# Third stage of a deformable convolution: every tile's corner sum kept in one tensor and transposed once

## The chip, the cores and the metric

The kernel runs on one core of one Trainium2 chip. The metric is the device time of one execution in microseconds (us); lower is better. Three executions without the profiler took 3535.86, 3537.91 and 3540.14 us, a median of 3537.91 us.

## The reference, cut to what matters

Two deformable convolutions follow each other, each with batch norm and leaky ReLU, and the input is added at the end. The first has one tap (a 1x1 kernel), the second nine (3x3). x is (8, 512, 52, 52) in float32, the middle tensor has 256 channels.

```
def _dcnv2(x, w_off, b_off, w, b, k, pad):
    om = conv(x, w_off, pad) + b_off
    oy, ox, mask = om[:, :P], om[:, P:2 * P], sigmoid(om[:, 2 * P:])
    val = bilinear(x, oy + base_y, ox + base_x) * mask      # 4 corners, weighted
    return einsum('ncphw,ocp->nohw', val, w) + b
h = bn_lrelu(_dcnv2(x, w_off1, b_off1, w1, b1, 1, 0), g1, bb1, m1, v1)
h = bn_lrelu(_dcnv2(h, w_off2, b_off2, w2, b2, 3, 1), g2, bb2, m2, v2)
return x + h
```

The bilinear value of a pixel at one tap is the sum of four corners, each corner's 256 channels times one weight.

## The kernel before, in words

The 21632 pixels are 169 tiles of 128. A first stage multiplies x with w1 (each factor split in a high and a low part) and writes table 1; a second samples table 1, makes h, writes it as table 2 and works out the offsets, corner weights and row numbers of all nine taps (plan2). Both end near 892 us of the profiled span, and the change doesn't touch them.

The third stage takes the tiles in groups of four (a super, 512 pixels) and each super in nine taps. There are 42 full supers, so 378 full taps, and then nine taps of a single tile. `r` numbers the taps. The five queues run the same list of taps (`position`, line 859): the first 18 taps (two supers) are written out, then a loop makes 20 passes of 18 taps, then the rest is written out. For one tap `r`:

- POOL gathers, for each of the four tiles, 128 rows of 4 x 256 numbers (the four corners) into one of 18 slots of `gather2` (L944). A slot comes free when DVE has made the tile's last corner step.
- ACT multiplies corner 0 by its weight into `val` (L959, four times), and for tile 2 alone corner 1 by its weight into `val_too` (L962). Between tile 1 and tile 2 it copies the transposed sums of tap r-2 out of PSUM in reduced precision: `val_hi` (L971, `upper`), once PE has transposed tap r-2 and finished the products of tap r-4.
- DVE adds the other corners with one SCALAR_TENSOR_TENSOR each (L1010, a "corner step"): first FIRST_PAIR (tiles 0 and 1, six steps), then `lower` of tap r-2 (L1017, `val_lo` = psum minus `val_hi`), then SECOND_PAIR (tiles 2 and 3, five steps). Tile 2 is summed in two parts: `val` gets corners 0 and 2, `val_too` corners 1 and 3. At taps 3 and 4 of a super two relus (L1024) and two residual adds (L1033) follow, for the super before.
- PE transposes the four tiles into `psum_val` (L1062, two halves of 128 channels each), when DVE's last step of the tap is done (`sampled`). For tile 2 each half takes two matmuls, one for `val` and one for `val_too`, and PSUM adds them up: ten instructions. Then come the 24 products of tap r-2 (L1076, `multiply`: 4 output blocks, 2 halves, 3 pairs of high and low parts) into `psum_acc`.
- When a super's nine taps are in, ACT takes the four blocks of `psum_acc` out to `z_sb` (L980, at its taps 3 and 4 of the next super, named EVACUATE), and PE's first product of the next super, in its step of tap 2, waits for that.
- SP loads plans and residual rows and stores the results.

The lines that set the order on DVE and the parts of tile 2:

```
def in_parts(r, i):
    return i == 2
FIRST_PAIR = ((0, 1), (1, 1), (0, 2), (1, 2), (0, 3), (1, 3))
SECOND_PAIR = ((3, 1), (2, 2), (3, 2), (2, 3), (3, 3))
EVACUATE = {3: {2: 0, 3: 1}, 4: {0: 2, 1: 3}}
RESIDUAL = {3: (0, 1), 4: (2, 3)}
```

A pair (i, q) is tile i, corner q.

## Time and profile before

| | before |
|---|---|
| median of 3 runs, us | 3537.91 |
| the profiled execution's own time, us | 3560.49 |
| its span, first to last instruction, us | 3558.7 |
| PE busy | 3205.6 us, 90% |
| DVE busy | 3041.0 us, 85% |
| ACT busy | 1743.8 us, 49% |
| POOL busy | 2299.7 us, 65% |
| mean granted TensorE clock | 0.964 of full speed |
| DMA | 1125.77 MB, mean 316 GB/s |

Busy is the time in which at least one instruction of the engine is under way, so it hides how close two instructions follow. The profiled execution took 22.6 us more than the median of the runs without the profiler; differences are worked out within it and then set against the median. In a timeline row "x5" are five instructions that follow without a gap; consecutive ones overlap a little, so the pace of a row "2.85 us x7" whose single instruction takes 0.48 is (2.85 - 0.48) / 6.

### The profile page before, as it was taken

Reading aid. Unit: us, or ns where it says so; the run is one execution under the profiler, and the core shown is the slowest. Engines: PE = TensorE matmul, PEld = TensorE weight load, DVE = VectorE, ACT = ScalarE, POOL = GpSimd, SP = SyncE. Lnnn points to the kernel's source line nnn. Section 1 sums busy time; section 2 is a strip of 40 time slices with the busy share of each in tenths; the row PEclk is TensorE's granted clock in tenths of the full one; section 3 lists DMA queues with packets and bytes.
Section 4 is the critical chain, followed back from the end, with each engine's and each line's share of the span. In section 5 each row is a group of like instructions: output and inputs, shape, how many; then the busy total and the mean of one; then the engine's idle time right before and its main releaser. Section 6 shows DMA issues by size and latency. Waiting matters only on the chain.

```text
span 3558.7 us, 60220 instructions
## 1 busy us (share of the span) xinstructions
PE 3205.6 (90%) x16754; PEld 2630.8 (74%) x16754; DVE 3041.0 (85%) x6454; ACT 1743.8 (49%) x3762; POOL 2299.7 (65%) x1727
## 2 busy tenths in 40 slices
PE   6996676776699999999999999999999999999999
PEld 6995443433588888888888788888878888887888
DVE  5546999998798898989898889889888988989894
ACT  3664656565344444444444444444444444444442
POOL 0002333331788788888888888878787887888781
PEclk8998988888799999999999999999999999999997
DMA  8997777775999989999999999899999989999991
GB/s 292 319 338 249 254 246 248 251 251 188 356 363 343 339 314 356 350 336 329 362 349 324 350 356 341 318 357 354 328 336 365 339 318 354 351 339 328 360 341 65
DMA packets 454538, 1125.77 MB, mean 316 GB/s; under 512 B 42812, under 2 KB 198972, under 8 KB 454256
## 3 DMA queue, kind: packets, MB, share of 16 engines
q0 software_dynamic: 244672, 891.09, 68.1%
q1 hardware_dynamic: 121520, 144.69, 12.0%
q10 hardware_dynamic: 88192, 88.61, 7.7%
q14 instruction: 139, 1.14, 0.1%
q8 instruction: 15, 0.25, 0.0%
HBM read 987.20 MB, written 137.04 MB: 316 GB/s over the span
## 4 chain that ended last, share of the span: by engine, by line
PE 64%; issue 4%; DVE 3%; ACT 2%; ACTq 0%; DMA 0%; DVEq 0%; POOL 0%; POOLq 0%
PE psum_acc L1076 55%; PE psum_val L1062 10%; DVE val L1010 2%; ACT val_too L962 1%; ACT val L959 1%; ACT z_sb L980 1%; DVE val_lo L1017 1%; DMA gather<-table,plan_in 0%; ACTq L979 0%; DMA plan_in<-plan 0%; POOL gather L944 0%; DVE val_too L1010 0%; ACTq L977 0%; ACT val_hi L971 0%; DVEq L1006 0%
## 5 line engine op out<-in xcount | busy, mean ns | idle before, releaser
L944 POOL DMA_INDIRECT gather<-table,plan_in x1521 | 2092.2, 1376 | 545.1 <-issue 347.4
L1010 DVE SCALAR_TENSOR_TENSOR val<-gather,plan_in,val 128x256 f32<-128x256 f32 x3807 | 1580.2, 476 | 122.7 <-ACT val L959 90.2
L1076 PE MATMUL psum_acc<-val_hi,w_hi 128*128 128x512 f32 (+1 forms) x3096 | 1241.5, 401 | 58.2 <-ACT z_sb L980 58.2
L1076 PE MATMUL psum_acc<-val_hi,w_lo 128*128 128x512 f32 (+1 forms) x3096 | 1214.3, 392 | 0.0
L1076 PE MATMUL psum_acc<-val_lo,w_hi 128*128 128x512 f32 (+1 forms) x3096 | 1209.7, 391 | 0.0
L971 ACT ACTIVATE val_hi<-psum_val 128x1024 fp32r<-128x1024 f32 (+1 forms) x387 | 391.7, 1012 | 1382.7 <-PE psum_acc L1076 1382.7
L1076 PEld LDWEIGHTS psum_acc<-val_hi,w_hi 128*128 128x128 f32 x3096 | 592.3, 191 | 174.8 <-ACT z_sb L980 65.2
L959 ACT ACTIVATE val<-gather,plan_in 128x256 f32<-128x256 f32 x1521 | 694.5, 499 | 27.1 <-DMA gather<-table,plan_in 27.0
L1076 PEld LDWEIGHTS psum_acc<-val_hi,w_lo 128*128 128x128 f32 x3096 | 591.3, 191 | 120.6
L1076 PEld LDWEIGHTS psum_acc<-val_lo,w_hi 128*128 128x128 f32 x3096 | 592.8, 191 | 108.2
L1017 DVE TENSOR_TENSOR val_lo<-psum_val,val_hi 128x1024 fp32r<-128x1024 f32 (+1 forms) x387 | 464.8, 1201 | 202.8 <-ACT val_hi L971 201.7
L1062 PE MATMUL psum_val<-ident,val 128*128 128x128 f32 x3042 | 484.7, 275 | 59.2 <-DVE val L1010 59.2
L1062 PEld LDWEIGHTS psum_val<-ident,val 128*128 128x128 f32 x3042 | 381.3, 142 | 116.2 <-DVE val L1010 34.2
L576 POOL DMA_INDIRECT area_b<-table,row_cur x169 | 197.2, 1167 | 324.5 <-DVE area_a L726 282.8
L665 ACT ACTIVATE area_b<-psum_t 32x384 f32<-32x384 f32 (+2 forms) x594 | 259.5, 437 | 135.9 <-PE psum_t L602 123.8
L602 PE MATMUL psum_t<-area_a,area_c 128*96 128x386 f32 (+2 forms) x792 | 270.4, 479 | 22.8 <-ACT area_b L665 20.8
L339 PE MATMUL psum_t<-w_hi,val_hi 128*128 128x260 f32 x676 | 201.3, 298 | 43.6 <-DVE val_lo L463 43.1
L602 PEld LDWEIGHTS psum_t<-area_a,area_c 128*96 128x96 f32 x792 | 126.8, 174 | 137.8 <-issue 67.4
L463 DVE TENSOR_TENSOR val_lo<-area_a,val_hi 128x512 fp32r<-128x512 f32 x169 | 115.5, 691 | 128.7 <-ACT val_hi L357 128.7
L726 DVE SCALAR_TENSOR_TENSOR area_a<-area_b,area_c,area_a 128x256 f32<-128x256 f32 x507 | 206.0, 478 | 0.0
L339 PE MATMUL psum_t<-w_lo,val_hi 128*128 128x260 f32 x676 | 195.7, 290 | 0.0
L339 PE MATMUL psum_t<-w_hi,val_lo 128*128 128x260 f32 x676 | 195.5, 289 | 0.0
(74 smaller groups left out, 2327.0 us busy)
## 6 DMA issues: line engine op xcount, KB each, us to landing
stage<-x SPq DMA_DIRECT2D x70, 512.0 KB, 6.6
out<-stage SPq DMA_DIRECT2D x140, 256.0 KB, 4.0
area_a<-x SPq DMA_DIRECT2D x68, 384.0 KB, 6.4
gather<-table,plan_in POOLq DMA_INDIRECT x1521, 6.4
table<-y_stage ACTq DMA_DIRECT2D x26, 896.0 KB, 6.7
table<-area_a ACTq DMA_DIRECT2D x26, 896.0 KB, 5.6
table<-y_stage ACTq DMA_DIRECT2D x26, 768.0 KB, 6.2
table<-area_a ACTq DMA_DIRECT2D x26, 768.0 KB, 5.8
```

What stands on the lines that cost most here:

```text
L339: last = nc.tensor.matmul(y_bank(j), a[:, X_SLOT[j], k, :], b[:, k, :], start=(k == 0 and a is x_hi and b is w1_hi), stop=(k == KT1 - 1 an ...
L576: nc.gpsimd.indirect_dma_start(gather1[:, j % SLOTS, :, :].rearrange("p q c -> p (q c)"), None, table1, bass.IndirectOffsetOnAxis(ap=row_c ...
L602: last = nc.tensor.matmul(conv_bank(u, n), woff_sb[:, kt, y, :], h_t[:, kt, at:at + n * P + 2], start=(kt == 0), stop=(kt == KT2 - 1))
L665: last = nc.scalar.activation(q_sb[rows, y, 0:n * P], conv_bank(3 * b + y, n)[rows, dx:dx + n * P], ACT.Copy)
L726: ins = nc.vector.scalar_tensor_tensor(out=v, in0=gather1[:, j % SLOTS, q, :], scalar=weights1[:, q, ds(nth, 1)], in1=bias1 if q == 0 else ...
L944: nc.gpsimd.indirect_dma_start(gather2[:, slot(r, i), :, :].rearrange("p q c -> p (q c)"), None, table2, bass.IndirectOffsetOnAxis(ap=row. ...
L959: last = nc.scalar.activation(val[:, r % VALS, i, :], gather2[:, slot(r, i), 0, :], ACT.Identity, scale=weight(r, i, 0))
L971: nc.scalar.activation(val_hi[:, r % 2, :, 0:n], psum_val[:, r % 2, :, 0:n], ACT.Identity).then_inc(hi_ready, 1)
L1010: nc.vector.scalar_tensor_tensor(out=v, in0=gather2[:, slot(r, i), q, :], scalar=weight(r, i, q), in1=v, op0=ALU.mult, op1=ALU.add).then_i ...
L1017: nc.vector.tensor_tensor(val_lo[:, r % 2, :, 0:n], psum_val[:, r % 2, :, 0:n], val_hi[:, r % 2, :, 0:n].bitcast(f32), ALU.subtract)\
L1062: last = nc.tensor.matmul(psum_val[:, r % 2, kt, i * P:(i + 1) * P], v, ident[:, :], start=(n == 0), stop=(n == len(parts) - 1), is_transp ...
L1076: last = nc.tensor.matmul(psum_acc[:, oc, 0:n], a[:, w, oc * P:(oc + 1) * P], b[:, r % 2, kt, 0:n], start=(w == 0 and a is w2_hi and b is ...
```

## The change

Tile 2 is treated as the other three. ACT no longer makes `val_too`; DVE makes three corner steps for tile 2, all into `val`, so SECOND_PAIR has six steps and each waits for the one before it on the same tile; PE transposes tile 2 with two instructions in place of four. The tensor `val_too` goes. Over the 378 full taps this is one corner step more on DVE, one scaling less on ACT and two transposing matmuls (with their weight loads) less on PE, each per tap. The nine taps of the last single tile are as before.

```
-        val_too = sb("val_too", [P, VALS, C_MID])
...
-            def in_parts(r, i):
-                return i == 2
...
-            SECOND_PAIR = ((3, 1), (2, 2), (3, 2), (2, 3), (3, 3))
+            SECOND_PAIR = ((2, 1), (3, 1), (2, 2), (3, 2), (2, 3), (3, 3))
...
-                    last = nc.scalar.activation(val[:, r % VALS, i, :], gather2[:, slot(r, i), 0, :],
-                                                ACT.Identity, scale=weight(r, i, 0))
-                    if in_parts(r, i):
-                        last = nc.scalar.activation(val_too[:, r % VALS, :], gather2[:, slot(r, i), 1, :],
-                                                    ACT.Identity, scale=weight(r, i, 1))
-                    last.then_inc(scaled, 1)
+                    nc.scalar.activation(val[:, r % VALS, i, :], gather2[:, slot(r, i), 0, :],
+                                         ACT.Identity, scale=weight(r, i, 0)).then_inc(scaled, 1)
...
-                        part = in_parts(r, i)
-                        if q == 1 or part and q == 2:
+                        if q == 1:
                             dve.wait_ge(scaled, units_to(it, r, i))
-                        elif not part:
+                        else:
                             dve.wait_ge(summed, count + sums.index((i, q - 1)) + 1)
-                        v = val_too[:, r % VALS, :] if part and q == 3 else val[:, r % VALS, i, :]
+                        v = val[:, r % VALS, i, :]
...
-                            parts = [val[:, r % VALS, i, ch]] + [val_too[:, r % VALS, ch]] * in_parts(r, i)
-                            for n, v in enumerate(parts):
-                                last = nc.tensor.matmul(psum_val[:, r % 2, kt, i * P:(i + 1) * P], v, ident[:, :],
-                                                        start=(n == 0), stop=(n == len(parts) - 1),
-                                                        is_transpose=True)
+                            last = nc.tensor.transpose(psum_val[:, r % 2, kt, i * P:(i + 1) * P],
+                                                       val[:, r % VALS, i, ch], ident[:, :])
```

PE's order at the place where the products of one tap end (L1076) and the transposes of the next follow (L1062), before:

```order
L1076 MATMUL psum_acc<-val_hi,w_lo 128x512
L1062 MATMUL psum_val<-ident,val 128x128 x5
L1062 MATMUL psum_val<-ident,val_too 128x128
L1062 MATMUL psum_val<-ident,val 128x128
L1062 MATMUL psum_val<-ident,val_too 128x128
L1062 MATMUL psum_val<-ident,val 128x128 x2
L1076 MATMUL psum_acc<-val_hi,w_hi 128x512
```

and with the change, in the loop (line numbers are those of the changed file; the ISA and REGISTER rows compute what a wait compares with):

```order
L1064 MATMUL psum_acc<-val_hi,w_lo 128x512
L1045 REGISTER_ALU
L1047 REGISTER_ALU
L1051 MATMUL psum_val<-ident,val 128x128 x8
L1060 ISA
L1064 MATMUL psum_acc<-val_hi,w_hi 128x512
```

Ten transposing instructions have become eight; nothing else on PE moved.

DVE's order around the second tap with relu and residual (L1024, L1033), before:

```order
L1010 SCALAR_TENSOR_TENSOR val<-gather,plan_in,val 128x256
L1024 SCALAR_TENSOR_TENSOR z_sb<-z_sb 128x512 x2
L1033 TENSOR_TENSOR stage<-z_sb,stage 128x512 x2
L1010 SCALAR_TENSOR_TENSOR val<-gather,plan_in,val 128x256 x6
L1017 TENSOR_TENSOR val_lo<-psum_val,val_hi 128x1024
L1010 SCALAR_TENSOR_TENSOR val<-gather,plan_in,val 128x256 x3
L1010 SCALAR_TENSOR_TENSOR val_too<-gather,plan_in,val_too 128x256
L1010 SCALAR_TENSOR_TENSOR val<-gather,plan_in,val 128x256 x7
L1017 TENSOR_TENSOR val_lo<-psum_val,val_hi 128x1024
```

and with the change:

```order
L1001 SCALAR_TENSOR_TENSOR val<-gather,plan_in,val 128x256 x6
L1015 SCALAR_TENSOR_TENSOR z_sb<-z_sb 128x512 x2
L1024 TENSOR_TENSOR stage<-z_sb,stage 128x512 x2
L1001 SCALAR_TENSOR_TENSOR val<-gather,plan_in,val 128x256 x6
L1008 TENSOR_TENSOR val_lo<-psum_val,val_hi 128x1024
L1001 SCALAR_TENSOR_TENSOR val<-gather,plan_in,val 128x256 x12
L1008 TENSOR_TENSOR val_lo<-psum_val,val_hi 128x1024
```

Between two `lower` instructions twelve corner steps stand where eleven stood; the relus and residual adds keep their place.

## Rows read from the trace of the kernel before

**Rows 1.** Windows, all engines: us, busy (count), PEclk, DMA share, GB/s.

```profile
1500.00:1800.00 300.00, 289.49 (x1490) 242.89 (x1489) 266.74 (x564) 142.62 (x281) 247.23 (x174) 1.00 0.93 338
```

**Rows 2.** The page's chain that ended last, shares by engine.

```profile
PE 64%; issue 4%; DVE 3%; ACT 2%; ACTq 0%; DMA 0%; DVEq 0%; POOL 0%; POOLq 0%
```

**Rows 3.** PE in order of time, two ordinary taps: start us, us.

```profile
2201.23 0.71 PE L1062 MATMUL psum_val<-ident,val 128*128 128x128 f32 x5
...
2207.81 0.71 PE L1062 MATMUL psum_val<-ident,val 128*128 128x128 f32 x5
```

**Rows 4.** The chain in order of time, the same tap: start us, us.

```profile
2202.49 5.48 PE psum_acc L1076 x24
2207.97 1.09 PE psum_val L1062 x10
```

**Rows 5.** DVE in order of time, the same tap: [idle before, releaser].

```profile
2202.49 1.23 DVE L1017 TENSOR_TENSOR val_lo<-psum_val,val_hi 128x1024 fp32r<-128x1024 f32 x1 [0.94 <-ACT val_hi L971]
...
2205.28 2.85 DVE L1010 SCALAR_TENSOR_TENSOR val<-gather,plan_in,val 128x256 f32<-128x256 f32 x7
```

**Rows 6.** DVE in order of time, from one pass of the loop to the next.

```profile
2258.34 2.46 DVE L1010 SCALAR_TENSOR_TENSOR val<-gather,plan_in,val 128x256 f32<-128x256 f32 x6 [4.92 <-ACT val L959]
2260.73 1.21 DVE L1017 TENSOR_TENSOR val_lo<-psum_val,val_hi 128x1024 fp32r<-128x1024 f32 x1
...
2266.22 1.21 DVE L1017 TENSOR_TENSOR val_lo<-psum_val,val_hi 128x1024 fp32r<-128x1024 f32 x1
```

**Rows 7.** Who waited for whom, 1500 to 3000 us: us, times, longest.

```profile
DVE val L1010 <- ACT val L959: 55.7, 33, 4.9
DVE val L1010 <- issue: 11.6, 3, 4.0
```

**Rows 8.** PE in order of time, the same passage.

```profile
2255.48 0.71 PE L1062 MATMUL psum_val<-ident,val 128*128 128x128 f32 x5
...
2264.05 0.76 PE L1062 MATMUL psum_val<-ident,val 128*128 128x128 f32 x5 [1.85 <-DVE val L1010]
```

**Rows 9.** PE in order of time, the change of super and the taps after it.

```profile
2277.27 0.71 PE L1062 MATMUL psum_val<-ident,val 128*128 128x128 f32 x5
...
2279.92 0.50 PE L1076 MATMUL psum_acc<-val_hi,w_hi 128*128 128x512 f32 x1 [1.39 <-ACT z_sb L980]
...
2285.50 0.71 PE L1062 MATMUL psum_val<-ident,val 128*128 128x128 f32 x5
...
2298.64 0.71 PE L1062 MATMUL psum_val<-ident,val 128*128 128x128 f32 x5
```

**Rows 10.** ACT in order of time, the same change of super.

```profile
2278.79 0.50 ACT L962 ACTIVATE val_too<-gather,plan_in 128x256 f32<-128x256 f32 x1
```

**Rows 11.** DVE in order of time, the same change of super.

```profile
2280.30 1.28 DVE L1010 SCALAR_TENSOR_TENSOR val<-gather,plan_in,val 128x256 f32<-128x256 f32 x3 [0.54 <-ACT val L959]
...
2287.07 1.22 DVE L1017 TENSOR_TENSOR val_lo<-psum_val,val_hi 128x1024 fp32r<-128x1024 f32 x1
...
2294.96 1.22 DVE L1017 TENSOR_TENSOR val_lo<-psum_val,val_hi 128x1024 fp32r<-128x1024 f32 x1
...
2297.68 2.46 DVE L1010 SCALAR_TENSOR_TENSOR val<-gather,plan_in,val 128x256 f32<-128x256 f32 x6
```

**Rows 12.** PE in order of time, ten passes of the loop apart.

```profile
1647.25 0.76 PE L1062 MATMUL psum_val<-ident,val 128*128 128x128 f32 x5 [1.45 <-DVE val L1010]
...
2881.37 0.76 PE L1062 MATMUL psum_val<-ident,val 128*128 128x128 f32 x5 [1.84 <-DVE val L1010]
```

**Rows 13.** PE in order of time, the loop's first return.

```profile
1154.81 1.21 PE L1062 MATMUL psum_val<-ident,val 128*128 128x128 f32 x5 [1.88 <-DVE val L1010]
...
1163.08 0.71 PE L1062 MATMUL psum_val<-ident,val 128*128 128x128 f32 x5
```

**Rows 14.** Windows at the loop's first return.

```profile
1154.00:1158.00 4.00, 3.19 (x13) 3.01 (x14) 4.00 (x9) 1.98 (x5) 3.09 (x2) 0.62 1.02 408
```

**Rows 15.** PE in order of time, the third stage's start.

```profile
922.19 1.33 PE L1062 MATMUL psum_val<-ident,val 128*128 128x128 f32 x5 [3.28 <-DVE val L1010]
```

## The prediction

> **What bounds the kernel now.** I read the page first, then windows of the third stage, then the chain of waits, and last each engine's timeline over two supers; the change touches only this stage. In a window of it PE is busy 289.5 of 300 us and DVE 266.7, at the full TensorE clock [rows 1]. The chain lies on PE for 64% and on DVE for 3% [rows 2]. PE's timeline shows why: an ordinary tap starts every 6.58 us [rows 3], and the chain splits it into 24 products in 5.48 us and ten transposes in 1.09 us, 6.57 together and 0.109 a transpose [rows 4]. Nothing stands idle between them.
>
> DVE is close behind. Its corner steps come every (2.85 - 0.48) / 6 = 0.395 us, and in an ordinary tap it waits 0.94 us for `val_hi`, ahead of `lower` [rows 5]. Where it doesn't wait, a tap of eleven steps and `lower` takes 2266.22 - 2260.73 = 5.49 us [rows 6]. So it has 6.57 - 5.49 = 1.08 us a tap to spare. Its last step of the tap ends at 2205.28 + 0.48 = 2205.76 [rows 5], and the transposes that need it start at 2207.81 [rows 3]: DVE leads by 2.05 us. More it cannot lead, since `lower` starts 1.26 us after PE's transposes of the tap before (2202.49 against 2201.23).
>
> Three things use the lead up:
> - **Return of the loop.** The reader is to see that DVE's first step of a pass comes 4.92 us after its last [rows 6], though the ACT result it is put down to had long been there. Such stalls come at every return, some labelled "issue" and near 4.0 us [rows 7]. PE's transposes were due at 2255.48 + 6.57 = 2262.05 and start at 2264.05 [rows 8], 2.00 late. By my account 4.92 - 1.08 - 2.05 = 1.79; the other 0.21 is the handover to a PE that stands still.
> - **Change of super.** The first product waits 1.39 us for ACT to empty `psum_acc`; from transposes to transposes it takes 2285.50 - 2277.27 = 8.23 us [rows 9], 1.66 more than a tap. DVE gains that as lead, less 0.54 us for which it waits on ACT [rows 11].
> - **Relu and residual.** Taps 3 and 4 take DVE 2294.96 - 2287.07 = 7.89 us [rows 11], 2.40 more than an ordinary tap, twice a super. The lead goes 2.05 + 1.66 - 0.54 = 3.17, then 3.17 + 1.08 - 2.40 = 1.85, then 0.53. The trace has 2298.64 [rows 9] less 2298.16 (2297.68 + 0.48) [rows 11] = 0.48. The account holds, and PE just escapes a stall here.
>
> As a whole: 18 taps of 6.57, two changes of 1.66 and one return of about 1.7 give 123.3 us a pass; ten passes took 2881.37 - 1647.25 = 1234.1 [rows 12].
>
> **The change, part by part.** It has 378 full taps, 41 supers whose relus fall in full taps, and 19 returns of the loop.
>
> *PE:* two transposes less, 0.218 us a tap, all of it where PE paces: 378 x 0.218 = **-82.4 us**. A tap becomes 6.35 us.
>
> *ACT:* one scaling less. It idles before each `val_hi` anyway, so 0 in ordinary taps. At the change of super it stands in the path: `val_too` starts 0.40 us before the emptying that PE waits for (2278.79 [rows 10]; the next starts at 2279.19). PE's shorter transposes take back 0.22 of it: 41 x 0.18 = **-7.4 us**. The 0.54 us wait of DVE should go as well. If ACT gained nothing here, this term is 0.
>
> *DVE:* one step more. Tile 2's three steps alternate with tile 3's, as those of tiles 0 and 1 already do, so I price it at the pace of rows 5, 0.395; the bounds are that and the 0.48 of one alone. A tap takes 5.89 us and leaves 0.47 to spare. The lead in ordinary taps becomes 6.35 - 1.26 - (2205.76 - 2202.49 + 0.395) = 1.43. Then:
> - After the change of super: 1.43 + 1.48 = 2.91. Tap 3's relus: 2.91 + 0.47 - 2.40 = 0.98. Tap 4's: 0.98 + 0.47 - 2.40 = -0.95. PE stalls for 0.95 + 0.21 = 1.16 us, where it did not before: 41 x 1.16 = **+47.6 us**. The bounds are 0 (if DVE got 1 us more lead than I see) and 41 x 1.9 (if the 0.54 wait on ACT stayed and the step cost 0.48).
> - At the return: 4.92 - 0.47 - 1.43 + 0.21 = 3.23 late instead of 2.00. The difference doesn't depend on how long the stall itself is: 19 x 1.23 = **+23.4 us**. After either stall DVE is back at full lead three or four taps later, before the next drain, so the two don't add to each other.
>
> *POOL and DMA:* no gather is added or moved. Slots come free in the same order, and the 18 slots are four and a half taps. The DMA share is 0.93 [rows 1]; a pass 1% shorter makes it 0.94. I price this at 0. SP's queue waits for DVE's count of finished tiles, which comes on time.
>
> So far -82.4 - 7.4 + 47.6 + 23.4 = **-18.8 us**.
>
> *The clock.* One return of the nineteen shows what a stall can also cost. After 1.88 us idle the transposes start at 1154.81 and the next at 1163.08 [rows 13], 8.27 us in place of 6.57, and the granted clock there is 0.62 of full speed [rows 14]: for some microseconds it was the lower of its two levels, 1.2 GHz. The price is 1.70 us. Eight other stalls of 1.7 to 1.9 us, such as those of rows 8 and 12, did not do it. After the change the stall is 3.0 us as the profile shows idle time; the nearest row has 3.28 us idle, at the stage's start, with the clock low after it [rows 15], though it was low before as well. The bounds are no more falls than now (0) and one at each return, 18 more, +30.6 us. I take seven more, between a row that falls once in nine at 1.9 us and one that lies above: **+11.9 us**. What the Trainium skill ("TensorE: MATMUL & The Clock Gate", section "Why this matters for your kernels") says speaks against this change: it warns that idle gaps between bursts of matmuls in the middle of a kernel put the array back to the lower clock. By that rule taken strictly each return would fall.
>
> The sum is -6.9 us on 3560.5 us of the profiled execution, 3553.6; on the median of the runs, 3537.9 - 6.9 = **3531 us**.
>
> **The rivals.**
> 1. *The clock falls no oftener than now.* For it: only one of the present stalls did it, and the new stalls at tap 5 (1.2 us) are short like those at the change of super, which never do. Then -18.8: 3519 us.
> 2. *PE stays the bound.* DVE would have to find 1.0 us of lead, so that taps 5 don't stall. Against it stands the account above, which gave the present 0.48 to within 0.05. Then -82.4 - 7.4 + 23.4 = -66.4: 3471 us.
> 3. *Slower: the clock falls at the loop's return.* The place is the first transposes of each pass, the price 1.70 us, and it decides from the eleventh extra fall on. With 18 more: -18.8 + 30.6 = +11.8: 3550 us.
> 4. *DVE's steps get slower.* The price of 12 steps a tap at 0.41 instead of 0.395 would be 0.18 a tap: the lead falls by 0.18, the spare time by 0.18, which makes 0.54 more at each tap 5 and 0.36 at each return, 41 x 0.54 + 19 x 0.36 = +29, so -6.9 + 29 = +22: 3560 us. Against it: the pace is 0.395 though POOL is busy 247 of 300 us [rows 1]. The Trainium skill ("SBUF — State Buffer", section "SBUF: two separate sides") has a rule for it: a DVE instruction with two inputs in SBUF and a GpSimd instruction that reads SBUF shut each other out. By that rule more steps would meet more gathers; the even pace in rows 5 doesn't show it.
> 5. *Nothing comes of it:* another limit, the transfers say, holds the pass at 123 us, or the steps fall otherwise than the order of instructions says. Against it: the DMA share is 0.93 at 338 GB/s over 300 us [rows 1] and reached 408 GB/s in a short stretch [rows 14], so the transfers have room. 3538 us.
>
> **How the numbers follow.** About 0.2%, 7 us, is what a measurement of this kernel can tell from no change. The forecast has 0.33, rival 1 0.27, rival 2 0.08, rival 3 0.14, rival 4 0.10, rival 5 0.08. Faster by over 0.2%: rivals 1 and 2 and a fifth of the forecast, 0.42. Within: most of the forecast and rival 5, 0.34. Slower: rivals 3 and 4, 0.24. The forecast's own range is 3524 to 3538; the range for 8 in 10 takes in rival 1 with an error of 11 us in the stalls at tap 5 (0.27 us each) and reaches past rival 3: 3508 to 3553. It leaves out rivals 2 and 4, 0.18 together.
>
> **What would show it.** Ordinary taps on PE every 6.35 us; corner steps still at 0.395; the wait ahead of `lower` down from 0.94 to about 0.3; a new PE wait for DVE of about 1 us at each tap 5; PE's wait at the loop's return near 3 us; `val_too` gone from ACT and the wait at the change of super nearly the same. A mean clock below 1.00 in windows of the third stage would be the clock term, and its first transposes at 0.2 us would count the falls. I am wrong if taps 5 don't stall, if DVE's steps have another pace, or if passes take more than 123.4 us with the clock at 1.00.

## The result, and the profile after

The changed kernel takes **3688.61 us** (median of 4 runs, 3683.6 to 3703.48) where the kernel before takes 3539.02 (4 runs on the same chip, 3535.86 to 3544.02): ratio 1.0428, 95% interval 1.0395 to 1.0461. It is 150 us slower; the forecast was 3531, the range 3508 to 3553. The kernel before takes one of two lengths from run to run (beside experiments 13 to 16, 15 of its 24 runs took 3533 to 3553 us at a mean granted clock of 0.968 to 0.971, and 9 took 3554 to 3575 at 0.960 to 0.965), and its profiled execution below is one of the longer kind.

| | before | after |
|---|---|---|
| the profiled execution's own time, us | 3560.49 | 3683.6 |
| its span, us | 3558.7 | 3681.8 |
| mean granted TensorE clock | 0.964 | 0.951 |
| mean tap, from the first to the last start of PE's transposes between 1200 and 3300 us | 6.84 us | 7.25 us |

378 full taps of 0.40 us more are 151 us, the whole difference: it is spread over the stage. The page of the kernel after: its busy times, its chain by engine and its costliest groups (busy, mean ns of one | idle before, what ended it):

```profile
PE 3175.2 (86%) x15998; PEld 2561.3 (70%) x15998; DVE 3181.9 (86%) x6832; ACT 1654.6 (45%) x3384; POOL 2484.1 (67%) x1727
...
issue 22%; PE 20%; DVE 15%; POOL 8%; DMA 7%; ACT 2%; DVEq 1%; POOLq 0%; ACTq 0%
...
L940 POOL DMA_INDIRECT gather<-table,plan_in x1521 | 2274.5, 1495 | 516.4 <-issue 406.0
L1001 DVE SCALAR_TENSOR_TENSOR val<-gather,plan_in,val 128x256 f32<-128x256 f32 x4563 | 1862.5, 476 | 235.7 <-ACT val L955 206.7
...
L955 ACT ACTIVATE val<-gather,plan_in 128x256 f32<-128x256 f32 x1521 | 719.9, 503 | 681.9 <-DMA gather<-table,plan_in 680.2
```

The same two groups of the kernel before, which the prediction did not read:

```profile
L944 POOL DMA_INDIRECT gather<-table,plan_in x1521 | 2092.2, 1376 | 545.1 <-issue 347.4
...
L959 ACT ACTIVATE val<-gather,plan_in 128x256 f32<-128x256 f32 x1521 | 694.5, 499 | 27.1 <-DMA gather<-table,plan_in 27.0
```

PE had 64% of the chain [rows 2] and now has 20%; POOL and DMA, at 0 before, have 15% together. ACT waited 27 us for gathers and now waits 680. A gather keeps POOL busy for 1495 ns in place of 1376. The corner step is unchanged at 476 ns.

The window that answers to [rows 1] (us, busy and count of PE, PEld, DVE, ACT, POOL, then the clock, DMA share, GB/s), after:

```profile
1500.00:1800.00 300.00, 273.21 (x1327) 225.09 (x1325) 268.39 (x574) 123.28 (x224) 249.70 (x166) 0.98 0.91 324
```

POOL looks idle for 50 of 300 us. It isn't: 249.70 / 166 is 1.504 us a gather, behind each lies an issue gap of 0.30 us (rows below), and 166 x 1.804 = 299.5 us. Fullness alone proves nothing, since the same sum for [rows 1] gives 174 x (1.421 + 0.30) = 299.4 us: POOL hardly stood still in the kernel before either. The difference is in who waits: between 1200 and 3300 us ACT waited 0 us for gathers before, and 512 us after. So now **POOL is the bound.** Four gathers make a tap: 4 x (1.495 + 0.30) = 7.18 us, the mean tap is 7.25. Before it is 4 x (1.376 + 0.30) = 6.70 against 6.84: with gathers of that length POOL had 2% to spare. The transfers are not the bound: their share of the DMA engines fell from 0.93 to 0.91.

Why a gather takes longer stands in two timelines of the same stretch. DVE after, in order of time (start us, us, ..., instructions in a row):

```profile
2234.58 4.83 DVE L1001 SCALAR_TENSOR_TENSOR val<-gather,plan_in,val 128x256 f32<-128x256 f32 x12
2239.33 1.22 DVE L1008 TENSOR_TENSOR val_lo<-psum_val,val_hi 128x1024 fp32r<-128x1024 f32 x1
2240.46 4.83 DVE L1001 SCALAR_TENSOR_TENSOR val<-gather,plan_in,val 128x256 f32<-128x256 f32 x12
2245.22 1.21 DVE L1008 TENSOR_TENSOR val_lo<-psum_val,val_hi 128x1024 fp32r<-128x1024 f32 x1
2246.35 4.83 DVE L1001 SCALAR_TENSOR_TENSOR val<-gather,plan_in,val 128x256 f32<-128x256 f32 x12
2251.20 1.23 DVE L1008 TENSOR_TENSOR val_lo<-psum_val,val_hi 128x1024 fp32r<-128x1024 f32 x1
```

and POOL after (with the idle time before each):

```profile
2234.65 1.22 POOL L940 DMA_INDIRECT gather<-table,plan_in  x1 [0.30 <-issue]
2236.18 4.05 POOL L940 DMA_INDIRECT gather<-table,plan_in  x1 [0.30 <-issue]
2240.53 1.22 POOL L940 DMA_INDIRECT gather<-table,plan_in  x1 [0.30 <-issue]
2242.06 4.05 POOL L940 DMA_INDIRECT gather<-table,plan_in  x1 [0.30 <-issue]
2246.42 1.22 POOL L940 DMA_INDIRECT gather<-table,plan_in  x1 [0.30 <-issue]
2247.94 4.06 POOL L940 DMA_INDIRECT gather<-table,plan_in  x1 [0.30 <-issue]
```

DVE goes through its taps without a pause, 2245.22 - 2239.33 = 5.89 us each. Each long gather begins among the twelve corner steps and ends 0.80 to 0.90 us after `lower` has begun (2236.18 + 4.05 = 2240.23; 2242.06 + 4.05 = 2246.11; 2247.94 + 4.06 = 2252.00), which is little less than the 0.94 us that an undisturbed gather takes in all. Two gathers fit in a tap where four are needed. Over 1200 to 3300 us, 247 of 1157 gathers last over 1.5 us; 123 of them end 0.90 us after the start of `lower`, 53 as long after the first corner step that follows the residual adds, and nearly all others 1.3 us after the start of a corner step. So `lower` is the commonest moment, but not the only one. A corner step has both its inputs in SBUF; `lower` has one in PSUM. Where DVE pauses, gathers are short; POOL in an ordinary tap of the kernel before:

```profile
2203.14 0.95 POOL L944 DMA_INDIRECT gather<-table,plan_in  x1 [0.30 <-issue]
2204.39 0.99 POOL L944 DMA_INDIRECT gather<-table,plan_in  x1 [0.30 <-issue]
2205.68 0.94 POOL L944 DMA_INDIRECT gather<-table,plan_in  x1 [0.30 <-DVE val_too L1010]
2206.93 1.22 POOL L944 DMA_INDIRECT gather<-table,plan_in  x1 [0.30 <-issue]
...
2264.33 2.79 POOL L944 DMA_INDIRECT gather<-table,plan_in  x1 [0.78 <-DVE val L1010]
2267.42 1.22 POOL L944 DMA_INDIRECT gather<-table,plan_in  x1 [0.30 <-issue]
2268.95 3.65 POOL L944 DMA_INDIRECT gather<-table,plan_in  x1 [0.30 <-issue]
```

The last three rows are the warning that lay in the trace of before: after the loop's return DVE catches up without its 0.94 us pause [rows 5, 6], and there gathers take 2.79 and 3.65 us. I read those places on DVE and PE and not on POOL.

So this is a cycle: gathers come late, ACT and with it DVE wait; in that pause POOL gets short gathers and catches up; then DVE catches up without a pause and starves POOL again. The waits of the kernel after, 1500 to 3000 us (us in total, times, longest):

```profile
ACT val L955 <- DMA gather<-table,plan_in: 397.4, 371, 4.0
...
DVE val L1001 <- ACT val L955: 118.5, 84, 5.4
PE psum_val L1051 <- DVE val L1001: 94.0, 51, 5.6
```

Where POOL keeps up, the stalls that I forecast for PE are there, in PE's order of time after: the wait at the change of super ([rows 9] had 1.39), and the new one at tap 5:

```profile
2217.79 0.50 PE L1064 MATMUL psum_acc<-val_hi,w_hi 128*128 128x512 f32 x1 [1.21 <-ACT z_sb L972]
...
2237.16 1.09 PE L1051 MATMUL psum_val<-ident,val 128*128 128x128 f32 x8 [0.95 <-DVE val L1001]
```

### The profile page after: what moved, and what is told of

It reads as the page before. It is cut to its first block, busy times and chain, and to the rows that moved or that the text cites. A ratio compares the mean times of both kernels' runs of the same rounds, so it can differ in the third digit from the quotient of the medians.

```text
span 3681.8 us, 59428 instructions
## 1 busy us (share of the span) xinstructions
PE 3175.2 (86%) x15998; PEld 2561.3 (70%) x15998; DVE 3181.9 (86%) x6832; ACT 1654.6 (45%) x3384; POOL 2484.1 (67%) x1727
## 4 chain that ended last, share of the span: by engine, by line
issue 22%; PE 20%; DVE 15%; POOL 8%; DMA 7%; ACT 2%; DVEq 1%; POOLq 0%; ACTq 0%
PE psum_acc L1064 17%; DVE val L1001 11%; POOL gather L940 8%; DMA gather<-table,plan_in 7%; PE psum_val L1051 3%; DVE val_lo L1008 3%; ACT val L955 1%; DVE z_sb L1015 1%; DVE stage L1024 1%; ACT val_hi L963 1%; DVEq L997 0%; ACT z_sb L972 0%; POOLq L937 0%; DVEq L999 0%; POOLq L938 0%
## 5 line engine op out<-in xcount | busy, mean ns | idle before, releaser
L940 POOL DMA_INDIRECT gather<-table,plan_in x1521 | 2274.5, 1495 | 516.4 <-issue 406.0
L1001 DVE SCALAR_TENSOR_TENSOR val<-gather,plan_in,val 128x256 f32<-128x256 f32 x4563 | 1862.5, 476 | 235.7 <-ACT val L955 206.7
L955 ACT ACTIVATE val<-gather,plan_in 128x256 f32<-128x256 f32 x1521 | 719.9, 503 | 681.9 <-DMA gather<-table,plan_in 680.2
L1051 PE MATMUL psum_val<-ident,val 128*128 128x128 f32 x3042 | 418.4, 282 | 193.9 <-DVE val L1001 193.6
L1051 PEld LDWEIGHTS psum_val<-ident,val 128*128 128x128 f32 x3042 | 361.5, 145 | 273.1 <-issue 197.2
```

The source lines that it names most:

```text
L940: nc.gpsimd.indirect_dma_start(gather2[:, slot(r, i), :, :].rearrange("p q c -> p (q c)"), None, table2, bass.IndirectOffsetOnAxis(ap=row. ...
L955: nc.scalar.activation(val[:, r % VALS, i, :], gather2[:, slot(r, i), 0, :], ACT.Identity, scale=weight(r, i, 0)).then_inc(scaled, 1)
L1001: nc.vector.scalar_tensor_tensor(out=v, in0=gather2[:, slot(r, i), q, :], scalar=weight(r, i, q), in1=v, op0=ALU.mult, op1=ALU.add).then_i ...
L1051: last = nc.tensor.transpose(psum_val[:, r % 2, kt, i * P:(i + 1) * P], val[:, r % VALS, i, ch], ident[:, :])
```

## The experiments

Theory A: DVE's corner steps, back to back, shut POOL's gathers out, since both read SBUF; a gather gets its turn when DVE pauses or works from PSUM. Rival B: the transfers are at their limit, and gathers wait for them. Rival C: DVE's and PE's own account is wrong, with or without the gathers. Each figure in brackets behind a median is the ratio to the kernel before on the same chip, with its 95% interval. Where the edit says "after", it is made to the changed kernel. Between experiments of different numbers the medians may lie on different chips, where the kernel before has 3538.7 to 3546.9 us; differences between them carry up to 8 us of that. The traces are of single executions, which lie up to 26 us from the median of their kernel.

**1. Eleven steps again.** After, with tile 2's corner 1 left out: DVE has the eleven steps of before, PE and ACT the work of after.

```
-SECOND_PAIR = ((2, 1), (3, 1), (2, 2), (3, 2), (2, 3), (3, 3))
+SECOND_PAIR = ((3, 1), (2, 2), (3, 2), (2, 3), (3, 3))
...
-if q == 1:
+if q == 1 or (i, q) == (2, 2):
```

> Eight transposes as in the changed kernel, but eleven corner steps: tile 2's corner 1 is left out. Theory A (shut out: while DVE issues steps with two SBUF inputs back to back, POOL's gather gets no turn before DVE pauses or runs lower): DVE has 0.86 us a tap to spare, so the pauses stay; gathers about 1.40 us on average, time 3460 to 3500. Theory B (the transfers are the limit and stretch the gathers): a shorter tap asks still more of them, not under 3540. Theory C (DVE just has too much work, POOL's longer gathers follow from that): 3455 to 3475, no stalls at tap 5.

Measured: 3520.67 us (0.9936, 0.991 to 0.9963); ACT waits 187.4 us for gathers between 1200 and 3300 us, the mean gather takes 1375 ns, a tap 6.75 us. Faster than before, but 21 to 61 us slower than theory A's span of 3460 to 3500, and above C's too. Without the step the whole loss is gone. Yet even so gathers are starved now and then, by a faster PE and hence shorter pauses of DVE: ahead of `lower` it idles 91 us between 1200 and 3300 us, where it idled 130 before.

**2 and 3. One more instruction, its input in PSUM or in SBUF.** Experiment 1, and ahead of each `lower` one TENSOR_TENSOR of 288 elements; the two kernels differ in one operand.

```
+nc.vector.tensor_tensor(spare[:, :], psum_val[:, r % 2, 0, 0:SPARE],
+                        val_hi[:, r % 2, 1, 0:SPARE].bitcast(f32), ALU.subtract)
```

```
+nc.vector.tensor_tensor(spare[:, :], val_hi[:, r % 2, 0, 0:SPARE].bitcast(f32),
+                        val_hi[:, r % 2, 1, 0:SPARE].bitcast(f32), ALU.subtract)
```

> As eleven (corner 1 of tile 2 left out), plus one TENSOR_TENSOR of 288 elements ahead of lower, with one input in PSUM and one in SBUF, into a spare tensor. DVE's work is that of the changed kernel. Theory A: POOL gets its turn beside that instruction, so clearly faster than extra_sbuf, by 2% or more: 3480 to 3580, gathers about 1.40 us. Theories B and C: the same time as extra_sbuf within 0.5%.

> As extra_psum, but both inputs of the extra instruction lie in SBUF; length and place are the same. Theory A: near the changed kernel, 3620 to 3700, gathers about 1.50 us. Theory B: also near it, and extra_psum with it. Theory C: near 3520 to 3690, and extra_psum the same within 0.5%.

Measured: 3619.73 us (1.0222, 1.0169 to 1.0274) with PSUM, 3703.09 us (1.0452, 1.0395 to 1.0509) with SBUF. The instruction takes DVE equally long. Its row in DVE's order of time, with PSUM:

```profile
2206.14 0.45 DVE L1011 TENSOR_TENSOR spare<-psum_val,val_hi 128x288 f32<-128x288 f32 x1
```

and with SBUF:

```profile
2208.24 0.45 DVE L1011 TENSOR_TENSOR spare<-val_hi 128x288 f32<-128x288 f32 x1
```

The page's row for the gathers, with PSUM:

```profile
L942 POOL DMA_INDIRECT gather<-table,plan_in x1521 | 2188.4, 1439 | 516.3 <-issue 378.2
```

and with SBUF:

```profile
L942 POOL DMA_INDIRECT gather<-table,plan_in x1521 | 2278.0, 1498 | 515.5 <-issue 400.6
```

0.45 us both times, and the kernels are 83 us apart. DVE's load is the same, PE's too, and the transfers are the same; what differs is where one input lies. The difference, 2.3%, is as theory A expected, and B and C wanted none above 0.5%; but with PSUM the kernel is 40 us above A's span (3480 to 3580) with gathers of 1439 ns, not 1400, and with SBUF 3 us above its span. The traces show the difference directly. With PSUM a long gather ends 0.91 us after the extra instruction has begun (2206.14 in the row above); POOL:

```profile
2202.81 4.24 POOL L942 DMA_INDIRECT gather<-table,plan_in  x1 [0.30 <-issue]
```

With SBUF the extra instruction of a like tap begins at 2214.09 and doesn't let the gather in; it ends 0.90 us after the start of `lower` (2211.34 + 4.02 = 2215.36). DVE and POOL:

```profile
2214.09 0.45 DVE L1011 TENSOR_TENSOR spare<-val_hi 128x288 f32<-128x288 f32 x1
2214.46 1.22 DVE L1013 TENSOR_TENSOR val_lo<-psum_val,val_hi 128x1024 fp32r<-128x1024 f32 x1
...
2211.34 4.02 POOL L942 DMA_INDIRECT gather<-table,plan_in  x1 [0.30 <-issue]
```

Of the gathers over 1.5 us between 1200 and 3300 us, 126 of 248 end so behind the extra instruction with PSUM, and 5 of 253 with SBUF, where 133 end so behind `lower`. Both instructions are a TENSOR_TENSOR at the same place, so a mere change in the kind of instruction is not what lets a gather in. These two runs speak most directly for A and against B and C. The kernel with SBUF has nearly the gather time (1498 ns) and the total of the changed one. The Trainium skill ("SBUF — State Buffer", section "SBUF: two separate sides") describes an exclusive lock on a port pair, taken by a DVE instruction with two SBUF inputs against a GpSimd instruction that reads SBUF. These two runs agree (3619.7 us with one input in PSUM, 3703.1 with both in SBUF); that the gather's own SBUF read (the row numbers) is what collides, no run here shows by itself.

**4. Half the bytes.** After; each gather brings 512 of its 1024 numbers, and the corner steps read the two corners that are there twice.

```
-gather2[:, slot(r, i), :, :].rearrange("p q c -> p (q c)"), None, table2,
+gather2[:, slot(r, i), 0:2, :].rearrange("p q c -> p (q c)"), None, table2,
...
-out=v, in0=gather2[:, slot(r, i), q, :], scalar=weight(r, i, q), in1=v,
+out=v, in0=gather2[:, slot(r, i), q % 2, :], scalar=weight(r, i, q), in1=v,
```

> The changed kernel with each gather bringing 512 of the 1024 numbers of a row (corners 2 and 3 are left out, corners 0 and 1 are used twice), so half the bytes. Theory A: as the changed kernel, 3640 to 3700, gathers still of 4 us where DVE doesn't pause. Theory B: back to 3530 or below, no long gathers. Theory C: as the changed kernel.

Measured: 3651.41 us (1.0274, 1.0215 to 1.0334). The page's row for gathers:

```profile
L940 POOL DMA_INDIRECT gather<-table,plan_in x1521 | 2248.3, 1478 | 515.7 <-issue 402.9
```

From issue to landing a gather now takes 3.7 us where it took 6.4 in the changed kernel, and POOL's time for it hardly moves. Some 400 MB less win 1%, gathers of up to 4.75 us remain, and ACT waits 848 us for gathers between 1200 and 3300 us, where it waited 512. B, which wanted 3530 us or less and no long gathers, is out.

**5. PE kept slow.** After; PE makes tile 2's transposes twice, so it has its ten instructions again.

```
+for _ in range(2 if i == 2 else 1):
+    last = nc.tensor.transpose(psum_val[:, r % 2, kt, i * P:(i + 1) * P],
+                               val[:, r % VALS, i, ch], ident[:, :])
```

> The changed kernel, but PE makes tile 2's two transposes twice, ten transposing instructions a tap as before; DVE as in the changed kernel. Theory A (shut out): POOL is the bound, so the two transposes cost little: 3680 to 3720, and nearly all of the loss lies in the twelfth corner step. Theory C (DVE has too much work beside a shorter PE tap): 3560 to 3600, below the changed kernel since DVE has 0.68 us a tap to spare against 6.57.

Measured: 3654.7 us (1.0306, 1.0273 to 1.034), below A's span and above C's: with **more** work on PE the kernel is 34 us faster than the changed one. A slower PE gives DVE longer pauses ahead of `lower` (between 1200 and 3300 us 76 us of them, in place of 43), and ACT's waits for gathers fall to 284 us from 512, at 1476 ns a gather. Theory A as I wrote it down had the time the same or a little longer; that the pauses would more than pay for the transposes I saw only from the result.

**6. Short steps.** After; a corner step works on 64 of its 256 channels.

```
+out=v[:, 0:CUT], in0=gather2[:, slot(r, i), q, 0:CUT], scalar=weight(r, i, q),
+in1=v[:, 0:CUT],
```

> The changed kernel with each corner step on 64 of the 256 channels (three quarters of the sums are left out), so twelve steps of about 0.2 us. The gathers and transfers are complete. Theory A: DVE pauses for over 2 us a tap, all gathers about 0.95 to 1.2 us, mean below 1.25, no wait for gathers, PE paces every tap at 6.35: 3440 to 3470. Theory B (transfers): POOL's gathers stay at 1.4 us or more, and not under 3530.

Measured: 3452.23 us (0.9752, 0.9715 to 0.979), as expected. The page's row for gathers:

```profile
L941 POOL DMA_INDIRECT gather<-table,plan_in x1521 | 1588.1, 1044 | 954.7 <-DVE val L1002 537.2
```

The gathers are short, POOL waits for free slots, and the transfers reach a share of 0.96 at a mean tap of 6.63 us: the DMA engines had room when the changed kernel crawled at 0.91.

**7. `lower` in two halves.** After; the second half of `lower` comes three corner steps after the first, so DVE turns to PSUM twice a tap.

```
-lower(it, r - 2)
+lower(it, r - 2, 0)
...
-sample(it, r, SECOND_PAIR)
+sample(it, r, SECOND_PAIR, 0, 3)
+lower(it, r - 2, 1)
+sample(it, r, SECOND_PAIR, 3, None)
```

> The changed kernel with lower in two halves of 512 elements, the second after three steps of the second pair: DVE's work grows by about 0.08 us a tap, and an instruction with an input in PSUM comes twice a tap. Theory A: where DVE doesn't pause, POOL gets a turn at each half, four gathers a tap of DVE in place of two: 3540 to 3640. Theories B and C: 3700 or more, since DVE only gets more work.

Measured: 3727.05 us (1.0494, 1.0447 to 1.0542), a plain miss for A, at a time that B and C had named. The two halves of one `lower` in DVE's order of time, where DVE doesn't pause:

```profile
2237.61 0.69 DVE L1009 TENSOR_TENSOR val_lo<-psum_val,val_hi 128x512 fp32r<-128x512 f32 x1
2239.39 0.69 DVE L1009 TENSOR_TENSOR val_lo<-psum_val,val_hi 128x512 fp32r<-128x512 f32 x1
```

and POOL's order of time in the same stretch:

```profile
2235.64 2.87 POOL L940 DMA_INDIRECT gather<-table,plan_in  x1 [0.30 <-DVE val L1001]
2238.82 1.09 POOL L940 DMA_INDIRECT gather<-table,plan_in  x1 [0.30 <-issue]
2240.21 1.08 POOL L940 DMA_INDIRECT gather<-table,plan_in  x1 [0.30 <-issue]
```

The longest gather again ends 0.90 us after a half has begun (2235.64 + 2.87 = 2238.51), and three gathers fit in a tap, not two. But over all its gathers the mean is 1534 ns, more than in the changed kernel. Where the time goes stands in DVE's rows at the loop's return, where every other kernel has at most one such stall and this one two:

```profile
1291.94 0.48 DVE L1001 SCALAR_TENSOR_TENSOR val<-gather,plan_in,val 128x256 f32<-128x256 f32 x1 [5.30 <-issue]
1297.04 2.07 DVE L1001 SCALAR_TENSOR_TENSOR val<-gather,plan_in,val 128x256 f32<-128x256 f32 x5 [4.62 <-issue]
```

At all 19 returns DVE stands a second time, for 4.4 to 4.7 us. PE's idle time ahead of the returns adds up to 160 us, against 79 in the changed kernel: 81 us more, where the profiled span is 59 longer. So outside the returns this kernel gained some 20 us (part of which may be turns that POOL got in the longer stalls), and the miss speaks against A only in part. Why DVE stands a second time no run here shows.

**8. Pauses.** After; the same twelve steps, tile 2's second step right behind its first. A step that needs the step just before it starts later, and DVE stands for a moment.

```
-SECOND_PAIR = ((2, 1), (3, 1), (2, 2), (3, 2), (2, 3), (3, 3))
+SECOND_PAIR = ((2, 1), (2, 2), (3, 1), (3, 2), (2, 3), (3, 3))
```

> The changed kernel with the second pair in the order (2,1) (2,2) (3,1) (3,2) (2,3) (3,3): twice a tap a step waits for the one right before it, about 0.12 us each, so DVE's tap grows by 0.25 us. Theory A: POOL gets in at these pauses, if a short one is enough: 3560 to 3660; if it needs a long one, 3700 to 3740. Theory C: 3730 or more.

Measured: 3619.83 us (1.0212, 1.0178 to 1.0246), 1.9% below the changed kernel, though twelve steps now take 5.11 us in place of 4.83. DVE's order of time:

```profile
2235.44 5.11 DVE L1001 SCALAR_TENSOR_TENSOR val<-gather,plan_in,val 128x256 f32<-128x256 f32 x12
```

The page's row for gathers:

```profile
L940 POOL DMA_INDIRECT gather<-table,plan_in x1521 | 1944.1, 1278 | 749.0 <-issue 360.6
```

The window of [rows 1]:

```profile
1500.00:1800.00 300.00, 275.15 (x1350) 228.16 (x1349) 280.27 (x589) 119.14 (x226) 214.99 (x170) 0.98 0.92 331
```

ACT no longer waits for gathers, and DVE (280 of 300 us busy) is the bound. The twelve steps take 0.28 us more, 106 us over 378 taps, and still the kernel wins 69 us: what was given away on the engine that looks busiest came back, and more, from the one that it starved.

**9. The account without starvation.** Experiment 1 with the pauses: eleven steps that take DVE as long as the changed kernel's twelve.

```
+SECOND_PAIR = ((2, 2), (2, 3), (3, 1), (3, 2), (3, 3))
```

> The kernel eleven (eight transposes, eleven steps, tile 2's corner 1 left out) with its second pair in the order (2,2) (2,3) (3,1) (3,2) (3,3): three steps that wait for the one right before them, 0.37 us a tap more for DVE. Theory A (POOL gets its turn in pauses of DVE, and lack of turns is what kept eleven from 3460): gathers from 1.38 us to below 1.25, time 3455 to 3485, 1 to 2% below eleven. Theory C (DVE's work counts, not POOL's turns): DVE has only 0.49 us a tap to spare, 3520 to 3540, as eleven or slower.

Measured: 3574.42 us (1.0091, 1.006 to 1.0122); the gathers fell as A expected, but both expected spans were missed. The page's row for gathers:

```profile
L940 POOL DMA_INDIRECT gather<-table,plan_in x1521 | 1575.3, 1036 | 1067.6 <-DVE val L1001 595.0
```

PE's order of time, at tap 5 and at the loop's return:

```profile
2239.03 1.09 PE L1051 MATMUL psum_val<-ident,val 128*128 128x128 f32 x8 [0.94 <-DVE val L1001]
...
2267.93 1.97 PE L1051 MATMUL psum_val<-ident,val 128*128 128x128 f32 x8 [3.30 <-DVE val L1001]
```

The window at that return (the clock is the 0.75):

```profile
2265.00:2270.00 5.00, 2.07 (x9) 2.08 (x10) 4.89 (x12) 2.28 (x5) 3.95 (x4) 0.75 0.59 177
```

This kernel is in its times what I had costed: ACT never waits for a gather between 1200 and 3300 us; DVE, where it doesn't wait, takes 5.86 to 6.00 us for a tap of eleven steps with pauses (from `lower` to `lower` 2241.20 - 2235.28 = 5.92, then 2247.06 - 2241.20 = 5.86), the changed kernel 5.89; PE's stalls are 0.94 and 3.30 us. The eight transposes at the return take 1.97 us in place of 1.04 with the clock at 0.75 there, and the tap behind it 7.8 to 8.0 us in place of 6.35. That happens at 15 of 19 returns. What this kernel takes over the one before, 36 us, is the PE and DVE account; what the changed one takes over this, 3688.6 - 3574.4 = 114 us, is starvation (by the ratios to the kernel before, 1.0428 less 1.0091, it is 119).

**10. Relus and residual adds spread.** After; one residual add a tap at taps 3 to 6 in place of two at taps 3 and 4.

```
-RESIDUAL = {3: (0, 1), 4: (2, 3)}
+RESIDUAL = {3: (0,), 4: (1,), 5: (2,), 6: (3,)}
...
-position(dve, step, after=5)
+position(dve, step, after=7)
```

> The changed kernel with one relu and one residual add at each of taps 3, 4, 5 and 6 of a super, in place of two of each at taps 3 and 4. My account of DVE's lead says that no tap then stalls PE for it (2.91, then 0.73 less at each of four taps). Theory A: POOL still finds too few turns while DVE catches up, but every residual add now waits for the relu right before it, which is a pause: 3610 to 3680. Theory C: 3530 to 3600, since only the burst of work was too much.

Measured: 3605.31 us (1.0183, 1.0134 to 1.0231), just below the expected span; gathers 1412 ns, ACT's waits for them 27 us. That fits A: without a pair of taps in which DVE falls 2.4 us behind each, it has less to catch up without a pause.

**11 and 12. Parts at even taps only.** Tile 2 in parts at even taps, three steps with pauses at odd ones; 12 also spreads the residual as in 10.

```
+def in_parts(r, i):
+    return i == 2 and r % 2 == 0
...
+SECOND_WHOLE = ((2, 1), (2, 2), (3, 1), (3, 2), (2, 3), (3, 3))
...
+sample(it, r, SECOND_WHOLE if r % 2 else SECOND_PAIR)
```

> A full version: tile 2 in two parts (before) at even taps, in three steps with the two pauses (2,1) (2,2) and (3,1) (3,2) at odd taps. PE's tap is 6.46 us on average, DVE's 5.81. Theory A: the pauses feed POOL, so PE stays the bound in most taps: 3500 to 3530, faster than before by up to 1%. Theory C: DVE has 0.65 us a tap to spare, 3535 to 3560.

> The kernel mixed with the relus and residual adds at taps 3, 4, 5 and 6, one of each. Theory A: the long stretch of DVE without a pause is broken up, so 10 to 20 us below mixed: 3490 to 3515. Theory C: as mixed within 0.3%.

Measured: 3550.97 us (1.0036, 1.0009 to 1.0063) and 3591.86 us (1.0158, 1.0105 to 1.0211). For 11, A's span was missed and C's (3535 to 3560) was met; for 12 both were missed. In 11 the gathers keep up (ACT waits 2.4 us between 1200 and 3300 us), so starvation is not what keeps it from A's time: PE still stalls at tap 5 (0.8 us) and 1.8 to 3.2 us at the returns, and what is gained on PE goes there. In 12 the gathers are short (1137 ns) and nobody waits for them, and the loss lies at the returns too: PE's idle time there is 2.8 to 4.0 us, 61 us in all against 46 in 11, and between 1200 and 3300 us the lower clock lengthens 15 taps, against 7. That is 15 us and 8 times 1.6 us, most of the 34 us between the two profiled spans. In experiment 10 spreading relieved POOL; here POOL needed no relief.

**13. Pauses in the kernel before.** A control: only the order of its five steps changes.

```
-SECOND_PAIR = ((3, 1), (2, 2), (3, 2), (2, 3), (3, 3))
+SECOND_PAIR = ((2, 2), (3, 1), (3, 2), (2, 3), (3, 3))
```

> The kernel before with its second pair in the order (2,2) (3,1) (3,2) (2,3) (3,3), so that two of its steps wait for the one right before them (0.25 us a tap more for DVE). Theory A (POOL gets its turns in pauses of DVE): gathers fall from 1.38 us to below 1.25, but PE paces the kernel before and no one waits for a gather there, so 3535 to 3565, the loop's return some 0.25 us dearer. If the shut-out already costs the kernel before time, 3510 to 3530.

Measured: 3568.68 us (1.0052, 1.0029 to 1.0076), 4 us above A's span. The gathers get shorter, and nobody needs it. The page's row:

```profile
L944 POOL DMA_INDIRECT gather<-table,plan_in x1521 | 1830.5, 1203 | 831.1 <-issue 405.0
```

DVE's longer taps make the stall at the loop's return 1.8 to 2.2 us, and the clock falls at 11 of 19 of them, where before it fell at one [rows 13]. Pauses pay only where the gathers are short of turns.

**14 and 15. Three steps at three taps of nine.** The kernel before with tile 2 in parts except at taps 1, 2 and 7 of a super, which have neither relus nor the change of super; 14 in the changed kernel's order, 15 with the pauses at those taps.

```
+WHOLE = (1, 2, 7)
+def in_parts(r, i):
+    return i == 2 and r % TAPS not in WHOLE
...
+SECOND_WHOLE = ((2, 1), (3, 1), (2, 2), (3, 2), (2, 3), (3, 3))
```

```
+SECOND_WHOLE = ((2, 1), (2, 2), (3, 1), (3, 2), (2, 3), (3, 3))
```

> A full version: tile 2 in three steps with two transposes at taps 1, 2 and 7 of a super, in two parts as before at the other six, where DVE's lead is short or about to be used. PE saves 126 x 0.218 = 27 us and by my account of the lead loses none of it again. If POOL keeps its turns: 3508 to 3522. If the shorter pauses at these taps already starve it: 3540 to 3580.

> The kernel three_taps with the two pauses (2,1) (2,2) and (3,1) (3,2) at its taps 1, 2 and 7, 0.25 us of DVE each. Theory A: the turns for POOL come back at these taps, 3505 to 3522, at or below three_taps. Without A: at or above three_taps, by up to 0.3%.

Measured: 3603.52 us (1.0154, 1.0102 to 1.0207) and **3527.27 us (0.9947, 0.9919 to 0.9975)**. For 14, both branches of the expectation (3508 to 3522, or 3540 to 3580) were too low, the starved one by 24 us; 15 is 5 us above A's span. One pair of steps changes places at a third of the taps, and 76 us go. The page's row for gathers in the order without pauses (14):

```profile
L947 POOL DMA_INDIRECT gather<-table,plan_in x1521 | 2177.8, 1432 | 516.5 <-issue 399.5
```

and among its waits, 1200 to 3300 us:

```profile
ACT val L962 <- DMA gather<-table,plan_in: 316.5, 304, 4.6
```

With the pauses (15) that wait is absent, and the page's row is:

```profile
L947 POOL DMA_INDIRECT gather<-table,plan_in x1521 | 2094.3, 1377 | 536.8 <-issue 404.5
```

Experiment 15 is the fastest kernel of the study that does the whole work, 0.5% faster than before.

**16 to 18. Emptying `psum_acc` earlier.** ACT takes out the first block of `psum_acc` before it scales tile 2 rather than after: added to 14 (16), to 15 (17) and to the kernel before (18).

```
+early = r % TAPS == 3 and i == 2
+if early and ahead(it, r - back):
+    evacuate(it, r - back, 0)
 if r < ALL_TAPS and i < tiles_of(r):
     scale(it, r, i)
```

> The kernel three_taps with ACT's first emptying of psum_acc ahead of its scaling of tile 2, 0.8 us earlier, so that PE's wait at the change of super is shorter: of the 0.8 the second block takes back 0.4. 41 x 0.4 = 16 us below three_taps; between 5 and 30 us below it.

> The kernel three_taps_pauses (3527 us) with ACT's first emptying of psum_acc moved ahead as in three_taps_evac, which was 24 us below its own base. The two edits act at different places, so 10 to 25 us below three_taps_pauses: 3500 to 3520, 0.7 to 1.3% faster than before. Should the earlier product use up DVE's lead at tap 5, which here has pauses to pay as well, it stays at 3525 to 3540.

> The kernel before with ACT's first emptying moved ahead, nothing else. My account: PE wins 0.8 - 0.4 = 0.4 us at each of 41 changes of super, 16 us; DVE's lead at tap 5 falls from 0.48 to about 0.1, just enough: 3515 to 3535. If gathers get short of turns by that: 3540 or more.

Measured: 3579.35 us (1.0096, 1.0059 to 1.0134), 24 below experiment 14 as expected, though the two intervals overlap; then 3557.29 us (1.0027, 1.0003 to 1.005), 30 above experiment 15 and above both spans expected for it; and 3573.33 us (1.0076, 1.0047 to 1.0105), the branch of the expectation in which the gathers get short of turns. In the kernel before, one ACT instruction made earlier lengthens the gathers from 1376 to 1412 ns and makes ACT wait 196 us for them between 1200 and 3300 us, where it waited for none. DVE's pauses ahead of `lower` there fall from 130 to 94 us: a shorter wait of PE takes pauses from DVE and turns from POOL. The kernel before sits right at the brink. For 17 the trace can't say what went wrong, since its profiled execution, 3531.76 us, is the fastest of its twelve and 26 us below their median.

How far POOL explains a tap, in eight of the kernels (mean gather of the page, mean tap from 1200 to 3300 us):

| kernel | 4 x (gather + 0.30) | mean tap | ACT waits for gathers there |
|---|---|---|---|
| eleven, 1 | 6.70 | 6.75 | 187 us |
| extra in PSUM, 2 | 6.96 | 7.01 | 380 us |
| three taps, 14 | 6.93 | 7.00 | 317 us |
| after | 7.18 | 7.25 | 512 us |
| extra in SBUF, 3 | 7.19 | 7.27 | 585 us |
| pauses, 8 | 6.31 | 7.02 | none |
| eleven with pauses, 9 | 5.34 | 6.90 | none |
| short steps, 6 | 5.38 | 6.63 | none |

The upper five rows agree within 0.08 us, as they must where POOL never stands still; that it also sets the pace there is told by the last column. In the lower three POOL stands idle at times, and another engine sets the pace.

## Why the prediction was wrong

**The step that failed** is the one on POOL and DMA: "no gather is added or moved. Slots come free in the same order ... I price this at 0". The order was right, and the slots never ran out. What I left out is that a gather has no fixed length: it lasts until DVE lets it in, and the change takes away the pauses in which it does. With POOL at 1.376 + 0.30 us a gather, 6.70 of a tap of 6.84, it had hardly room for that. I took POOL's 247 of 300 busy us in [rows 1] for slack of 53; 174 issue gaps of 0.30 us are 52 of them. The term measured 114 us (experiment 9 against the changed kernel).

**Rival 4** named the rule and the wrong loser. I asked whether DVE's steps get slower, found them even in [rows 5], and gave it 0.10. They stay even (4.83 - 0.48) / 11 = 0.395 in the changed kernel too. It was the gather that waited, and the row to look at was POOL's.

**PE, change of super, DVE.** These held. Experiment 9 has PE taps of 6.34 us (forecast 6.35), a stall of 0.94 at tap 5 (forecast 1.16, "about 1 us" as idle time), a wait at the return of 3.30 ("near 3 us"). By the account without the clock a pass is 18.8 / 20 = 0.9 us shorter than 123.4, that is 122.5. Experiment 9 measures 124.2: 1.3 of the 1.7 us between them are the clock (15 of 19 returns at 1.6), and the other 0.4 lie mostly at the return, which without a fall costs some 3.4 us where 2.9 were in the sum.

**The clock** was under-priced. I took seven more falls, 11.9 us, from a row that falls once in nine (the trace has seven other stalls of its size, not eight). Experiment 9 has 14 more, at 1.6 us each. The runs count, by the idle time of PE ahead of a tap's transposes from 1100 us on (a fall is a tap that is lengthened as in experiment 9, with the clock for part of it at the lower of its two levels, 1.2 GHz: its mean granted clock is below 0.97): 1.0 to 1.8 us, 0 of 9 before, 0 of 38 in experiment 8 and 0 of 15 in experiment 6; 1.8 to 2.2 us, 1 of 5 before, 11 of 19 in experiment 13, 4 of 8 in experiment 15, 1 of 1 in experiment 8 and 0 of 1 in experiment 6; 2.2 to 2.9 us, 2 of 3 in experiment 6 and 0 of 1 in experiment 8; from 2.9 us, 15 of 19 in experiment 9, 18 of 18 in experiment 8, 19 of 19 after. Rival 3, a fall at each return, was nearer for stalls of 3 us; at eleven extra falls it only breaks even (18.7 of 18.8 us). The Trainium skill ("TensorE: Matmul & The Clock Gate", section "Why this matters for your kernels"), which the prediction quoted, warns of idle gaps between bursts of matmuls. The trace agrees for the stalls from 2.9 us on, 52 of 56; of the 62 under 1.8 us none was followed by a fall.

**Set against the median.** I added the difference within the profile to the median of the runs. For experiment 9 the spans of the profiled executions differ by 3571.0 - 3558.7 = 12.3 us and the medians by 36: the profiled execution of the kernel before is 22 us longer than its median, that of experiment 9 is 2 shorter than its own. So the 12 us can be set against my -6.9: the seven further falls (11 us) and 19 returns that are 0.4 us dearer each (8 us) make up the difference of 19. The other 24 us are the distance of these profiled executions from their medians, and why the kernel before has it stays open.

**What else stays open:** exactly which moments of DVE give POOL a turn (half of the long gathers end behind something other than `lower`, and gathers of 1.22 us are let in behind the first corner step after `lower`), why DVE stands twice at the returns of experiment 7, and why experiment 17 is slower than 15.

## What to carry to other kernels

Before an instruction with two SBUF inputs is added to DVE beside software-generated gathers, read POOL's timeline where DVE already runs without a pause: the gathers' lengths there (2.8 to 3.7 us beside 0.95 elsewhere) tell what the change will make the rule. Count the issue gap as POOL's time, 0.30 us behind each of these gathers. If gathers are the bound, reorder dependent steps so that DVE stands for a moment: 0.28 us of DVE a tap bought 69 us here, and where nobody waited for gathers (experiment 13) two such pauses cost 0.5%, some 20 us.

## What the runs showed of the hardware that I had not expected

- The length of one and the same kind of gather goes from 0.94 to 4.06 us with what DVE does beside it (4.75 in experiment 4); its bytes hardly matter to POOL (1495 against 1478 ns at half of them).
- Moving one 128x288 input of a 0.45 us DVE instruction from PSUM to SBUF cost 83 us over the kernel.
- Of the two, the gather alone pays: the corner step's mean stays at 476 ns.
- More work on PE made the kernel faster (3654.7 against 3688.6 us), and one instruction moved earlier on ACT made it slower (3573.33 against 3544.47): in both the pauses of DVE ahead of `lower` moved with it (43 to 76 us, and 130 to 94).
- Cutting one DVE instruction in two made DVE stand a second time, for 4.4 to 4.7 us, at each of the loop's 19 returns (experiment 7).
